# Spreads of attention weights as pairs of 32 x 64 matmuls, with a second copy of the values whose images are swapped

## The chip, the cores and the metric

The kernel runs on one core of one Trainium2 chip. The metric is the time of an execution on the device in microseconds (us); what is quoted is the median of several runs.

## The reference, cut to what matters

Two layers on x of 4 images, 64 channels, 32 x 32 pixels. The first is a deformable attention with 8 heads and 4 points:

```
v = (q @ W_value + b_value).reshape(B, Nq, HEADS, d)
off = (q @ W_off + b_off).reshape(B, Nq, HEADS, LEVELS, POINTS, 2)
attn = softmax(q @ W_attn + b_attn) over the 4 points
loc = ref + off / norm;  ix = loc_x * W - 0.5;  iy = loc_y * H - 0.5
sampled = bilinear samples of v at (ix, iy), zero outside
out = (sampled * attn).sum over points
out = out @ W_out + b_out + q
```

The second is a 3 x 3 convolution of the signs of its result with the signs of the weights (times their mean size), a batch normalization over all pixels, a residual and a PReLU. The signs need the whole attention, and the normalization needs the whole convolution.

## The kernel before, in words

Two images share the 128 partitions (PAIR = 2, 64 channels each), so there are G = 2 groups; `yh` is the upper or lower half of the pixels, 512 each. Offsets are small, so each pixel samples among 4 x 4 neighbours. A **tap** is one neighbour of one half: t from 0 to 31, in rows of four (row n = t // 4, the neighbour's line; column t % 4). For each tap:

- `attend` (VectorE, once a row) multiplies the turned probabilities by the vertical hat: `ps_ay`, in PSUM. ScalarE's `copy_ay` brings it to SBUF as `ays`.
- `weight` multiplies `ays` by the horizontal hat: the tap's weight, 128 rows (group, image, head, point) by 512 pixels. GpSimd makes 30 of the 32 (line 754, tile `ap`, four buffers), VectorE the first two (tile `a`).
- `spread` (TensorE, line 431) sums the points and copies each head's weight to its 8 channels, by four matmuls with 0/1 matrices, one per group and image. Each reads 64 rows, of which 32 are of its image. It writes `ps_w`, two buffers of two banks. For group 1 the images come out crossed, and `vpad` holds the values crossed too.
- `product` (VectorE, line 850) multiplies by the shifted window of the padded values `vpad`: `prod`, 8 buffers.
- a **unit** of `project` (TensorE, line 451) applies W_out and adds into `ps_out`: the unit of a tap, or ("sum", n), the sum of two products of a row that GpSimd's `pair_sum` makes with an adding DMA (line 760).

Every engine runs its own list in the order of the program; semaphores join them. TensorE's list has spread t, then what `UNITS_AFTER[t]` names, then spread t + 1. `carry_x` (line 444) starts an accumulation with x itself, once a half, and `turn` (line 419) transposes the probabilities. After the last unit ScalarE makes the signs of the lower half (line 680), TensorE convolves (line 483), VectorE takes statistics, and ScalarE, VectorE and GpSimd make the result. A flag (line 544) tells whether an offset was too large for 16 taps; it isn't here.

Of the kernel before, what the change touches and what calls it, by code (L numbers as in the profile page):

```python
# [20 lines left out]
PAIR = 2  # L21
G = B // PAIR
P = PAIR * C
YH = 2
# [12 lines left out]
SUMMED = range(ROWS - 1)  # L37
# [65 lines left out]
def deformable_attention_then_binary_conv(nc, x, const, w_in, w_out, params, w_conv, w_abs, out):  # L103
    ctx = ExitStack()
    with ctx:
# [35 lines left out]
        PR = 8  # L141
# [4 lines left out]
        flag = sb("flag", [1, 2])  # L146
# [30 lines left out]
        ps_flag = bank[6]  # L177
# [16 lines left out]
        s_vlow = sem("lower_values_stored")  # L194
        s_pos = sem("position_parts_ready")
# [9 lines left out]
        s_att = sem("probs_turned")  # L205
        s_ay = sem("ay_ready")
        s_a = sem("tap_weights_ready")
        s_ayc = sem("ay_copied")
# [72 lines left out]
        def v_window(g, yh, ky, kx):  # L281
# [44 lines left out]
        def units_of(n):  # L326

            first = TAPS * n
            if n == ROWS - 1:
                return [("tap", t) for t in range(first, first + TAPS)]  # L330
            return [("tap", first + 2), ("tap", first + 3), ("sum", n)]

        UNITS_AFTER = {6: [("tap", 2), ("tap", 3)], 7: [("sum", 0)], 17: [("tap", 15), ("sum", 3)], 18: [], 20: [],
                       21: [("tap", 18), ("tap", 19)], 31: [("tap", 28), ("tap", 29)]}
        for n in range(2, ROWS):
            for column in range(3):
                UNITS_AFTER.setdefault(TAPS * n + column, units_of(n - 1)[column:column + 1])
        UNITS = [unit for n in range(ROWS) for unit in units_of(n)]
        UPPER_UNITS = sum(len(units_of(n)) for n in range(TAPS))
# [11 lines left out]
        def quadrant(i, g):  # L351

            return slice(i * C, (i + 1) * C), slice((i ^ g) * C, (i ^ g) * C + C)
# [28 lines left out]
        def _(pe):  # L382
# [32 lines left out]
            def turn(yh):  # L415

                pe.wait_ge(s_prob, yh + 1)
                for n in range(NCH):
                    mm = pe.transpose(ps_att[:, n * P:(n + 1) * P], prob[:, yh, n * P:(n + 1) * P], cst[:, c_eye:c_eye + P])  # L419
# [103 lines left out]
            for t in range(NT * YH):  # L523
# [10 lines left out]
                if t == NT + 4:  # L534
                    carry_x(1)
# [510 lines left out]
```

## Time and profile before

| | us |
|---|---|
| median of 3 runs | 95.57 (95.44 to 96.04) |
| profiled execution | 95.7 |
| its span in the trace | 93.9 |
| TensorE busy | 76.6 |
| VectorE busy | 65.0 |
| GpSimd busy | 51.0 |
| ScalarE busy | 47.9 |

The span is what the trace covers; the profiled execution's time is 1.8 us more. PE is TensorE (PEld its weight loads), DVE VectorE, ACT ScalarE, POOL GpSimd, SP the sync engine, and a q behind a name its queue. In the trace each fp32 matmul shows as two records, so a spread's four matmuls are eight. A record of a matmul ends later than the next can begin (they are pipelined), so costs are taken from the distance between starts, or from the chain.

### The profile page before, as it was taken

To read this page: it belongs to the slowest core of one execution; us is meant where nothing else is said; L and a number is where in the kernel's file an instruction comes from. 1 tells how busy PE (TensorE), PEld (TensorE's weight loads), DVE (VectorE), ACT (ScalarE), POOL (GpSimd) and SP (SyncE) were. 2 spreads that over 40 slices of the span, in tenths; PEclk is the share of its full clock that TensorE was granted. 3 is DMA by queue.
4 is the path that set the end of the run, shared out by engine and by line. 5 is a ranking of instruction groups with operands and counts; after the bars stand their busy time and mean duration, and the time that the engine had idled before them with its cause. 6 is when DMAs were issued, how large, how long until landed. Compare 5 with 4: busy or idle time off the path is not lost.

```text
span 93.9 us, 1689 instructions
## 1 busy us (share of the span) xinstructions
PE 76.6 (82%) x648; PEld 33.0 (35%) x648; DVE 65.0 (69%) x81; ACT 47.9 (51%) x76; POOL 51.0 (54%) x47
## 2 busy tenths in 40 slices
PE   5999799879999999999997799999999999220000
PEld 4547074112246544333331355333333345010000
DVE  2624695995999664987973954997776408659930
ACT  2200899988689990399708950220000039419900
POOL 7920000059999999999998568899800000005000
PEclk9999999999999999999999999999999999996555
DMA  1998000000083083470924700910910000000095
GB/s 27 249 358 327 6 0 0 0 0 7 0 168 56 0 168 63 82 141 0 178 49 84 143 7 3 194 30 0 195 35 0 0 7 0 0 0 0 14 257 180
DMA packets 3209, 7.10 MB, mean 76 GB/s; under 512 B 512, under 2 KB 1024, under 8 KB 3200
## 3 DMA queue, kind: packets, MB, share of 16 engines
q0 software_dynamic: 1008, 3.67, 20.6%
q1 hardware_dynamic: 1904, 2.89, 9.8%
q10 hardware_dynamic: 288, 0.43, 1.5%
q8 instruction: 5, 0.08, 0.4%
q14 instruction: 4, 0.03, 0.1%
HBM read 2.27 MB, written 1.05 MB: 35 GB/s over the span
## 4 chain that ended last, share of the span: by engine, by line
PE 67%; ACT 15%; DVE 7%; issue 4%; POOL 3%; ACTq 1%; DVEq 0%; POOLq 0%
PE banks L431 27%; PE banks L451 23%; PE banks L444 4%; ACT tab L609 3%; ACT hat L614 3%; PE banks L483 3%; PE banks L501 3%; POOL ap L754 2%; ACT prod L734 2%; PE banks L404 2%; PE banks L396 2%; ACT prod L736 2%; DVE bns L957 1%; ACT sg L680 1%; ACT u L602 1%
## 5 line engine op out<-in xcount | busy, mean ns | idle before, releaser
L754 POOL TENSOR_TENSOR ap<-ays,hat 128x512 f32<-128x512 f32 x30 | 40.4, 1564 | 17.4 <-ACT ays L623 15.7
L850 DVE TENSOR_TENSOR prod<-banks,vpad 128x1024 f32<-128x1024 f32 (+1 forms) x33 | 38.6, 1187 | 11.7 <-PE banks L431 11.7
L431 PE MATMUL banks<-ap,cst 64*64 64x512 f32 x240 | 33.9, 596 | 1.3 <-DVE prod L850 1.1
L451 PE MATMUL banks<-prod,wo 64*64 64x512 f32 x200 | 27.8, 590 | 0.0
L431 PEld LDWEIGHTS banks<-ap,cst 64*64 64x64 f32 x240 | 10.1, 132 | 17.2 <-issue 9.4
L451 PEld LDWEIGHTS banks<-prod,wo 64*64 64x64 f32 x200 | 9.9, 133 | 11.5 <-issue 9.6
L779 POOL TENSOR_SCALAR prod<-prod,prm,st 128x512 f32<-128x512 f32 x2 | 1.5, 768 | 17.7 <-ACT st L728 17.7
L623 ACT ACTIVATE ays<-banks 128x512 f32<-128x512 f32 x8 | 4.7, 588 | 9.9 <-DVE banks L822 9.9
L609 ACT ACTIVATE tab<-u,cst 128x1024 f32<-128x1024 f32 x8 | 8.9, 1141 | 0.2
L680 ACT ACTIVATE sg<-banks,st 128x512 bf16<-128x512 f32 x2 | 1.3, 687 | 14.9 <-PE banks L451 14.9
L614 ACT ACTIVATE hat<-tab 128x1024 f32<-128x1024 f32 x8 | 8.3, 1050 | 0.1
L760 POOL DMA_DIRECT2D prod<-prod x7 | 7.5, 1077 | 0.4 <-issue 0.4
L822 DVE TENSOR_TENSOR banks<-banks,hat 128x512 f32<-128x512 f32 x8 | 5.5, 691 | 0.9 <-PE banks L419 0.9
L483 PE MATMUL banks<-sg,wcb 64*64 64x512 bf16 (+2 forms) x84 | 4.6, 350 | 0.2 <-ACT sg L680 0.2
L404 PEld LDWEIGHTS banks<-win,xs 128*128 128x128 f32 x32 | 3.9, 196 | 1.1 <-issue 1.1
L635 ACT ACTIVATE ex<-lsub 128x512 f32<-128x512 f32 x1 | 0.6, 631 | 6.9 <-DVE lsub L791 6.9
L390 PE MATMUL banks<-xs,win 128*64 128x512 f32 x16 | 4.1, 611 | 0.0
L404 PE MATMUL banks<-win,xs 128*128 128x64 f32 x32 | 4.0, 277 | 0.0
L444 PE MATMUL banks<-xs,cst 64*64 64x512 f32 x16 | 3.8, 590 | 0.0
L501 PE MATMUL banks<-ones 128*128 128x256 f32 x6 | 2.9, 661 | 1.0 <-POOL ones L742 1.0
L396 PE MATMUL banks<-prm,top_ones 128*128 128x512 f32 x4 | 3.0, 846 | 0.7 <-ACT u L602 0.7
L787 DVE TENSOR_REDUCE lmax<-banks 128x128 f32<-128x512 f32 x2 | 1.4, 686 | 3.1 <-PE banks L404 3.1
(81 smaller groups left out, 74.0 us busy)
## 6 DMA issues: line engine op xcount, KB each, us to landing
prod<-prod POOLq DMA_DIRECT2D x7, 512.0 KB, 4.8
xs<-x_dram SPq DMA_DIRECT2D x3, 256.0 KB, 4.9
out_dram<-prod SPq DMA_DIRECT2D x4, 128.0 KB, 2.6
out_dram<-prod SPq DMA_DIRECT2D x2, 256.0 KB, 2.6
wcf<-w_conv_dram SPq DMA_DIRECT2D x1, 288.0 KB, 5.2
wab<-w_abs_dram SPq DMA_DIRECT2D x1, 288.0 KB, 5.2
xs<-x_dram ACTq DMA_DIRECT2D x1, 256.0 KB, 4.1
cst<-const_dram SPq DMA_DIRECT2D x1, 227.0 KB, 5.0
```

What stands on the lines that cost most here:

```text
L404: mm = pe.matmul(ps_log[yh][:, at:at + C], xs[:, g, q:q + P], wp[:, 2, :], start=False, stop=(n == NCH - 1 and g == G - 1), skip_group_che ...
L431: mm = pe.matmul(ps_w[t % 2][rows_out, g, :], sel_of(g)[rows_in, rows_out], weights_at(t)[rows_in], start=True, stop=True)
L444: mm = pe.matmul(ps_out[g][rows_of_i], cst[rows_of_i, c_eye + i * C:c_eye + (i + 1) * C], chunk(xs, g, yh)[rows_of_i], start=True, stop=Fa ...
L451: mm = pe.matmul(ps_out[g][rows_out], wo[rows_in, rows_in], source[rows_in, g, :], start=False, stop=last, skip_group_check=True)
L483: mm = pe.matmul(ps_y[yh][g][rows_out, first_row * W:last_row * W], wcb[rows_in, ky * K + kx, :], sg[rows_in, g, y0:y0 + last_row - first_ ...
L501: pe.matmul(bank[6][:, 0:2 * P], ones[:], ones[:].unsqueeze(1).to_broadcast([P, 2, P]), start=True, stop=True)
L609: nc.scalar.activation(tab[:, n % 2], u[:, :, yh, :], ACT.Abs, bias=cst[:, c_tap + k:c_tap + k + 1]).then_inc(s_abs, 1)
L614: nc.scalar.activation(hat[:, yh, :, k, :], tab[:, n % 2], ACT.Relu, bias=1.0, scale=-1.0).then_inc(s_hat, 1)
L754: pool.tensor_tensor(ap[:, j % RAP, :], ays[:, t // TAPS % RY, :], hat[:, yh, 0, kx, :], ALU.mult).then_inc(s_ap, 1)
L760: pool.dma_start(prod[:, t % PR], prod[:, (t + 1) % PR], accum_op=ALU.add).then_inc(s_s2[n % 2], 16)
L822: nc.vector.tensor_tensor(ps_ay[:], ps_att[:], hat[:, yh, 1, ORDER[row], :], ALU.mult).then_inc(s_ay, 1)
L850: nc.vector.tensor_tensor(by_half_row(prod[:, t % PR, g, :]), by_half_row(ps_w[t % 2][:, g, :]), v_window(g, yh, ky, kx), ALU.mult).then_i ...
```

## The change

- **Spreads**: each of the four matmuls of a tap reads only the 32 rows of its group and image, a 32 x 64 tile. Taps 2 to 29 go in pairs. The second tap of a pair is "swapped": its images come out in the other halves of the partitions, so that the eight matmuls of a pair have eight different tiles. Its product reads `vswap`, a copy of `vpad` with the halves exchanged, which SP's queue makes with four DMAs, and its unit projects by the other quadrants. Units of both kinds are told apart by `is_swapped`; where the kind changes TensorE waits for its last unit.
- `ps_w` has three buffers, `prod` twelve, `ays` three. Pair sums add columns 0 and 2 of rows 0 to 5. `UNITS_AFTER` is a new table, and `carry_x(1)` comes three taps later.
- **Row factors**: ScalarE copies the turned probabilities to SBUF (`att`) once per half; `attend` reads them there (but for row 0) and writes `ays` in SBUF; `copy_ay` is gone. `turn(1)` has a spread's PSUM buffer and goes in before spread 10, which waits for ScalarE's copy.
- The flag's sum is moved from VectorE at the end to ScalarE in the middle.

```diff
-SUMMED = range(ROWS - 1)
+SUMMED = range(ROWS - 2)
+SPREADS = [(0,), (1,)] + [(t, t + 1) for t in range(2, ROWS * TAPS - 2, 2)] + [(ROWS * TAPS - 2,), (ROWS * TAPS - 1,)]
+SWAPPED = [pair[1] for pair in SPREADS if len(pair) == 2]
+TURN_AFTER = 9
...
+        vswap = sb("vswap", [P, G, VP, 2, SEG])
...
-        RY = 2
+        RY = 3
         ays = sb("ays", [P, RY, HALF])
+        att = sb("att", [P, YH, HALF])
...
-        PR = 8
+        PR = 12
...
-        ps_w = [banks[0], banks[1]]
+        ps_w = [banks[0], banks[1], banks[3]]
+        NW = len(ps_w)
         ps_out = [bank[4], bank[5]]
-        ps_att = bank[6]
-        ps_ay = bank[7]
+        turn_slot = (TURN_AFTER + 1) % NW
+        ps_att = [bank[6], ps_w[turn_slot][:, 0, :]]
...
+            yh, ky, kx = tap_of(t)
             y0 = yh * RH + ky + yh
-            return vpad[:, g, y0:y0 + RH, :, kx:kx + HW].rearrange("p g y a x -> p g (y a) x")
+            return (vswap if t in SWAPPED else vpad)[:, g, y0:y0 + RH, :, kx:kx + HW].rearrange("p g y a x -> p g (y a) x")
...
+        UNITS_AFTER = {7: [("tap", 3)], 9: [("tap", 1), ("sum", 0)], 11: [("tap", 5), ("tap", 7)], 13: [("sum", 1)],
+                       15: [("tap", 9), ("tap", 11)], 17: [("sum", 2)], 19: [("tap", 13), ("tap", 15)], 21: [("sum", 3)],
+                       25: [("sum", 4)], 27: [("tap", 17), ("tap", 19), ("tap", 21)], 29: [("sum", 5), ("tap", 24)],
+                       30: [("tap", 23), ("tap", 25)], 31: [("tap", 27)]}
+        UNITS_AT_END = [("tap", 29), ("tap", 26), ("tap", 28), ("tap", 30), ("tap", 31)]
+        UNITS = [unit for t in sorted(UNITS_AFTER) for unit in UNITS_AFTER[t]] + UNITS_AT_END
+        UPPER_UNITS = UNITS.index(("sum", 3)) + 1
...
-        def quadrant(i, g):
-
-            return slice(i * C, (i + 1) * C), slice((i ^ g) * C, (i ^ g) * C + C)
+        def quadrant(i, g, swapped=False):
+
+            j = i ^ g ^ swapped
+            return slice(i * C, (i + 1) * C), slice(j * C, (j + 1) * C)
...
+            for yh in range(YH):
+                sp.wait_ge([s_vp, s_vlow][yh], 2)
+                at = slice(yh * VP // YH, (yh + 1) * VP // YH)
+                for i in range(PAIR):
+                    rows_in, rows_out = quadrant(i, 1)
+                    sp.dma_start(vswap[rows_out, :, at], vpad[rows_in, :, at]).then_inc(s_vswap[yh], 16)
...
+                if t == 2:
+                    pe.wait_ge(s_attc, 1)
+                if t == TURN_AFTER + 1:
+                    pe.wait_ge(s_attc, 2)
+                if t >= NW:
+                    pe.wait_ge(s_p, products_done(t - NW, G - 1))
                 for g in range(G):
-                    rows_in = slice(g * C, (g + 1) * C)
                     for i in range(PAIR):
-                        rows_out = slice(i * C, (i + 1) * C)
-                        mm = pe.matmul(ps_w[t % 2][rows_out, g, :], sel_of(g)[rows_in, rows_out], weights_at(t)[rows_in],
+                        rows_in = slice(g * C + i * HP, g * C + (i + 1) * HP)
+                        lhs = cst[rows_in, c_sel + g * P + (i ^ g) * C:c_sel + g * P + (i ^ g) * C + C]
+                        mm = pe.matmul(ps_w[t % NW][quadrant(i, g, t in SWAPPED)[1], g, :], lhs, weights_at(t)[rows_in],
...
+                    pe.wait_ge(s_ov, 4)
+                    pe.matmul(ps_flag[0:1, 0:4], ones[:, 0:1], over_sum[:], start=True, stop=True).then_inc(s_fps, 1)
...
+                swapped = is_swapped(unit)
+                at = UNITS.index(unit)
+                if at and is_swapped(UNITS[at - 1]) != swapped:
+                    pe.wait_ge(s_acc, at)
+                mm = project_image(source, swapped, 0, last)
...
-            for t in range(NT * YH):
-                spread(t)
+            for taps in SPREADS:
+                for t in taps:
+                    spread(t)
...
-                if t == NT + 4:
+                if t == TURN_AFTER:
+                    pe.wait_ge(s_p, products_done(t + 1 - NW, G - 1))
+                    turn(1)
+                if t == NT + 7:
...
-                if t == 2 * TAPS + 1:
-                    pe.wait_ge(s_ay, TAPS)
-                    turn(1)
-                if t == 28:
-                    pe.wait_ge(s_ov, 4)
-                    pe.wait_ge(s_ay, ROWS)
-                    pe.matmul(ps_flag[0:1, 0:4], ones[:, 0:1], over_sum[:], start=True, stop=True).then_inc(s_fps, 1)
...
-            def copy_ay(n):
-
-                act.wait_ge(s_ay, n + 1)
-                if n == 0:
-                    act.wait_ge(s_a, DVE_COLUMNS[0])
-                if n >= RY:
-                    act.wait_ge(s_ap, sum(TAPS - c for c in DVE_COLUMNS[:n - RY + 1]))
-                nc.scalar.activation(ays[:, n % RY, :], ps_ay[:], ACT.Identity).then_inc(s_ayc, 1)
+            def copy_turned(yh):
+
+                act.wait_ge(s_att, yh + 1)
+                if yh == 0:
+                    act.wait_ge(s_ay, 1)
+                nc.scalar.activation(att[:, yh, :], ps_att[yh][:], ACT.Identity).then_inc(s_attc, 1)
...
+            act.wait_ge(s_fps, 1)
+            nc.scalar.activation(flag[:, 4:8], ps_flag[0:1, 0:4], ACT.Identity, accum_out=flag[:, 0:1]).then_inc(s_f1, 1)
...
-                pool.wait_ge(s_ayc, t // TAPS + 1)
+                pool.wait_ge(s_ay, t // TAPS + 1)
...
-                pool.wait_ge(s_p, products_done(t + 1, G - 1))
-                pool.dma_start(prod[:, t % PR], prod[:, (t + 1) % PR], accum_op=ALU.add).then_inc(s_s2[n % 2], 16)
+                pool.wait_ge(s_p, products_done(t + 2, G - 1))
+                pool.dma_start(prod[:, t % PR], prod[:, (t + 2) % PR], accum_op=ALU.add).then_inc(s_s2[n % 2], 16)
...
-                dve.wait_ge(s_att, yh + 1)
                 if n:
-                    dve.wait_ge(s_ayc, n)
+                    dve.wait_ge(s_attc, yh + 1)
+                    source = att[:, yh, :]
+                else:
+                    dve.wait_ge(s_att, 1)
+                    source = ps_att[0][:]
+                if n >= RY:
+                    dve.wait_ge(s_ap, sum(TAPS - c for c in DVE_COLUMNS[:n - RY + 1]))
                 wait_for_hat(dve, yh, ORDER[row])
-                nc.vector.tensor_tensor(ps_ay[:], ps_att[:], hat[:, yh, 1, ORDER[row], :], ALU.mult).then_inc(s_ay, 1)
+                nc.vector.tensor_tensor(ays[:, n % RY, :], source, hat[:, yh, 1, ORDER[row], :], ALU.mult).then_inc(s_ay, 1)
...
+                if t in SWAPPED:
+                    dve.wait_ge(s_vswap[0], 16 * PAIR)
+                    if yh or ky == TAPS - 1:
+                        dve.wait_ge(s_vswap[1], 16 * PAIR)
...
-                    nc.vector.tensor_tensor(by_half_row(prod[:, t % PR, g, :]), by_half_row(ps_w[t % 2][:, g, :]),
-                                            v_window(g, yh, ky, kx), ALU.mult).then_inc(s_p, 1)
+                    nc.vector.tensor_tensor(by_half_row(prod[:, t % PR, g, :]), by_half_row(ps_w[t % NW][:, g, :]),
+                                            v_window(t, g), ALU.mult).then_inc(s_p, 1)
```

TensorE's list around the last spreads, before (MATMUL x4 is one tap's spread at L431 or one unit at L451):

```order
L451 MATMUL banks<-prod,wo 64x512 x4
L431 MATMUL banks<-ap,cst 64x512 x4
L451 MATMUL banks<-prod,wo 64x512 x4
L431 MATMUL banks<-ap,cst 64x512 x4
L451 MATMUL banks<-prod,wo 64x512 x12
L483 MATMUL banks<-sg,wcb 64x512 x12
L451 MATMUL banks<-prod,wo 64x512 x4
```

The same place in the changed kernel, from the pair (26,27) on (spreads at L453, units at L477, the convolution at L513):

```order
L453 MATMUL banks<-ap,cst 64x512 x8
L477 MATMUL banks<-prod,wo 64x512 x12
L453 MATMUL banks<-ap,cst 64x512 x8
L477 MATMUL banks<-prod,wo 64x512 x8
L453 MATMUL banks<-ap,cst 64x512 x4
L477 MATMUL banks<-prod,wo 64x512 x8
L453 MATMUL banks<-ap,cst 64x512 x4
L477 MATMUL banks<-prod,wo 64x512 x20
L513 MATMUL banks<-sg,wcb 64x512 x12
L477 MATMUL banks<-prod,wo 64x512 x4
```

Between the last spread and the convolution stand three units before, five now, and two units stand ahead of that spread where there was one.

VectorE's list in rows 1 and 2, before (products at L850, `attend` at L822):

```order
L850 TENSOR_TENSOR prod<-banks,vpad 128x1024
L822 TENSOR_TENSOR banks<-banks,hat 128x512
L850 TENSOR_TENSOR prod<-banks,vpad 128x1024 x2
L796 TENSOR_REDUCE lsum<-ex 128x128
L822 TENSOR_TENSOR banks<-banks,hat 128x512
```

And in the changed kernel (products at L878, `attend` at L849), with what each waits for:

```order
L878 TENSOR_TENSOR prod<-banks,vpad 128x1024 [waits spread_ready]
L849 TENSOR_TENSOR ays<-att,hat 128x512 [waits hats_ready,turned_probs_copied]
L878 TENSOR_TENSOR prod<-banks,vpad 128x1024 [waits spread_ready]
L878 TENSOR_TENSOR prod<-banks,vswap 128x1024 [waits spread_ready,swapped_upper_values_in]
L818 TENSOR_REDUCE lsum<-ex 128x128 [waits exp_ready]
L849 TENSOR_TENSOR ays<-att,hat 128x512 [waits hats_ready,turned_probs_copied]
```

The places of `attend` stay; its operands move from PSUM to SBUF, and every second product reads `vswap`.

## Rows read from the trace of the kernel before

**Rows 1.** The page: busy time and share per engine, chain that ended last by engine and line.
```profile
PE 76.6 (82%) x648; PEld 33.0 (35%) x648; DVE 65.0 (69%) x81; ACT 47.9 (51%) x76; POOL 51.0 (54%) x47
...
PE 67%; ACT 15%; DVE 7%; issue 4%; POOL 3%; ACTq 1%; DVEq 0%; POOLq 0%
PE banks L431 27%; PE banks L451 23%; PE banks L444 4%; ACT tab L609 3%; ACT hat L614 3%; PE banks L483 3%; PE banks L501 3%; POOL ap L754 2%; ACT prod L734 2%; PE banks L404 2%; PE banks L396 2%; ACT prod L736 2%; DVE bns L957 1%; ACT sg L680 1%; ACT u L602 1%
```

**Rows 2.** Waits: engine and line, released by, us in total, times, longest.
```profile
DVE prod L850 <- PE banks L431: 11.7, 17, 1.9
...
PEld banks L431 <- POOL ap L754: 7.5, 11, 1.9
```

**Rows 3.** The chain in time: start us, us, what; fp32 spreads and units are x8.
```profile
22.44 1.09 PE banks L431 x8
...
26.10 1.72 PE banks L444 x8
...
34.69 0.86 PE banks L451 x8
35.55 0.59 PE banks L419 x4
36.14 1.02 PE banks L431 x8
...
75.04 0.66 PE banks L483 x12
75.70 0.93 PE banks L451 x8
...
76.65 0.58 ACT sg L680
```

**Rows 4.** GpSimd's timeline: start us, us, instruction; in brackets idle time before it.
```profile
19.87 5.00 POOL L754 TENSOR_TENSOR ap<-ays,hat 128x512 f32<-128x512 f32 x4 [14.64 <-ACT ays L623]
24.81 1.00 POOL L760 DMA_DIRECT2D prod<-prod  x1
...
28.08 1.33 POOL L771 TENSOR_TENSOR prob<-ex,lrec 128x512 f32<-128x512 f32 x1
29.14 2.74 POOL L754 TENSOR_TENSOR ap<-ays,hat 128x512 f32<-128x512 f32 x2
...
37.15 1.41 POOL L760 DMA_DIRECT2D prod<-prod  x1
37.76 5.80 POOL L754 TENSOR_TENSOR ap<-ays,hat 128x512 f32<-128x512 f32 x4
...
50.48 2.50 POOL L754 TENSOR_TENSOR ap<-ays,hat 128x512 f32<-128x512 f32 x2 [0.26 <-PE banks L431]
```

**Rows 5.** VectorE's timeline, the same columns.
```profile
12.20 0.69 DVE L805 TENSOR_TENSOR prob<-ex,lrec 128x512 f32<-128x512 f32 x1
...
22.36 2.46 DVE L850 TENSOR_TENSOR prod<-banks,vpad 128x1024 f32<-128x1024 f32 x2 [0.96 <-PE banks L431]
...
27.06 0.94 DVE L800 RECIPROCAL lrec<-lsum 128x128 f32<-128x128 f32 x1
...
37.29 1.23 DVE L850 TENSOR_TENSOR prod<-banks,vpad 128x1024 f32<-128x1024 f32 x1 [1.23 <-PE banks L431]
38.44 0.69 DVE L822 TENSOR_TENSOR banks<-banks,hat 128x512 f32<-128x512 f32 x1
39.03 2.35 DVE L850 TENSOR_TENSOR prod<-banks,vpad 128x1024 f32<-128x1024 f32 x2
```

**Rows 6.** Timeline of all engines, 2.8 to 5.6 us: VectorE's cast beside GpSimd's memset.
```profile
3.19 2.07 DVE L862 CAST pos_b<-prm 128x32 bf16<-128x32 f32 x1 [1.80 <-DMA prm<-params_dram]
3.20 2.02 POOL L744 MEMSET sg<- 128x2312 bf16 x1
```

**Rows 7.** The page: DMA issues, KB each, us to landing.
```profile
xs<-x_dram SPq DMA_DIRECT2D x3, 256.0 KB, 4.9
```

**Rows 8.** Window: us, busy time (instructions) of PE, PEld, DVE, ACT, POOL, granted clock, DMA.
```profile
50.30:67.80 17.50, 16.43 (x144) 6.64 (x136) 13.36 (x13) 6.21 (x15) 14.41 (x12) 1.00 0.45 86
```

More of the change, by code:

```diff
@@ L145, in deformable_attention_then_binary_conv @@
         overs = sb("overs", [P, 2, HALF])
-        flag = sb("flag", [1, 2])
+        flag = sb("flag", [1, 8])
         flagi = sb("flagi", [1, 1], I32)
@@ L176, in deformable_attention_then_binary_conv @@
         ps_log = [bank[7], bank[4]]
-        ps_flag = bank[6]
+        ps_flag = bank[4]
         ps_pair = bank[4]
@@ L324, in products_done, with is_swapped, last_read @@
             return t + 1 + (g if t == NT * YH - 1 else 0)
[L326 to L339, printed above, removed]
+        def is_swapped(unit):
+            return unit[0] == "tap" and unit[1] in SWAPPED
+        def last_read(t):
+            row, column = divmod(t, TAPS)
+            if row in SUMMED and column == 0:
+                return ("sum", row)
+            return ("tap", t)
+        UNITS_AFTER = {7: [("tap", 3)], 9: [("tap", 1), ("sum", 0)], 11: [("tap", 5), ("tap", 7)], 13: [("sum", 1)],
[5 more added lines that the diff above has]
+        UPPER_UNITS = UNITS.index(("sum", 3)) + 1
         def units_done(unit, g=G - 1):
@@ L440, in carry_x @@
                     pe.wait_ge(s_x1, 2)
-                for g in range(G):
+                    pe.wait_ge(s_ov, 4)
+                    pe.matmul(ps_flag[0:1, 0:4], ones[:, 0:1], over_sum[:], start=True, stop=True).then_inc(s_fps, 1)
+                for g in reversed(range(G)):
+                    if yh and g == 0:
+                        pe.wait_ge(s_f1, 1)
                     for i in range(PAIR):
@@ L446, in carry_x, with project_image @@
                 mm.then_inc(s_carry, 1)
-            def project_image(source, g, last):
+            def project_image(source, swapped, g, last):
                 for i in range(PAIR):
-                    rows_in, rows_out = quadrant(i, g)
+                    rows_in, rows_out = quadrant(i, g, swapped)
                     mm = pe.matmul(ps_out[g][rows_out], wo[rows_in, rows_in], source[rows_in, g, :], start=False, stop=last,
@@ L473, in project @@
                     pe.wait_ge(s_p, products_done(n, 1))
-                project_image(source, 1, last).then_inc(s_acc, 1)
+                project_image(source, swapped, 1, last).then_inc(s_acc, 1)
             def convolve_row(yh, ky, first_row, last_row):
@@ L537, in _ @@
                     project(unit)
-                if t == 2 * TAPS + 1:
-                    pe.wait_ge(s_ay, TAPS)
-                    turn(1)
-                if t == 28:
-                    pe.wait_ge(s_ov, 4)
-                    pe.wait_ge(s_ay, ROWS)
-                    pe.matmul(ps_flag[0:1, 0:4], ones[:, 0:1], over_sum[:], start=True, stop=True).then_inc(s_fps, 1)
-            project(UNITS[-2])
-            pe.wait_ge(s_f1, 1)
+            for unit in UNITS_AT_END[:-1]:
+                project(unit)
+            pe.wait_ge(s_p, products_done(NT * YH - 3, G - 1))
             pe.wait_ge(s_wc, 1)
@@ L766, in _ @@
                     weight(TAPS * (n + 1) + column)
-                    if column == 1:
+                    if column == 2 and n in SUMMED:
                         pair_sum(n)
@@ L830, in weight @@
                     dve.wait_ge(s_w, taps_of(False)[i - RA] + 1)
-                nc.vector.tensor_tensor(a[:, i % RA, :], ps_ay[:], hat[:, yh, 0, kx, :], ALU.mult).then_inc(s_a, 1)
+                nc.vector.tensor_tensor(a[:, i % RA, :], ays[:, t // TAPS % RY, :], hat[:, yh, 0, kx, :], ALU.mult).then_inc(s_a, 1)
             def product(t):
@@ L836, in product @@
                     dve.wait_ge(s_vlow, 2)
+                if t in SWAPPED:
+                    dve.wait_ge(s_vswap[0], 16 * PAIR)
+                    if yh or ky == TAPS - 1:
+                        dve.wait_ge(s_vswap[1], 16 * PAIR)
                 if t >= PR:
                     old = t - PR
[L839 to L844 removed]
+                    row, column = divmod(old, TAPS)
+                    if row in SUMMED and column == 2:
+                        dve.wait_ge(s_s2[row % 2], 16 * (row // 2 + 1))
                     else:
[L846 removed]
+                        dve.wait_ge(s_acc, units_done(last_read(old)))
                 dve.wait_ge(s_w, t + 1)
```

30 lines of the change are left out of this document (6 added, 24 removed).

## The prediction

> **What bounds the kernel now.** I read the page first, for its busy shares and its chain [rows 1]: the tensor engine is busy for 82% of the span, carries 67% of the chain, and half of the chain is two lines, the spreads (L431) and the projections of `project` (L451). Then the waits, for who feeds whom [rows 2]: VectorE waits 11.7 us for spreads, TensorE's weight loads wait 7.5 us for GpSimd's `ap`. Then the chain in time [rows 3]. One spread of a tap is 8 records in 0.86 us, one projected unit is 8 records in 0.86 us, and `carry_x` is 1.72 us, since its two images use the same two quadrants. From 22.44 to 76.65 us (the first `sign` of the lower half) the chain is almost only these. After that comes a tail of 95.7 − 76.65 = 19.05 us that the change leaves alone; the profiled execution took 95.7 us, 0.13 over the median of the runs, and my sum is made against it.
>
> Two other engines are close behind. GpSimd's stretch [rows 4]: four tap weights from 19.87 to the DMA issue at 24.81, 1.235 us each; the issue of a pair sum costs it 0.61 (37.15 to 37.76); `prob` of the lower half costs 1.06 (28.08 to 29.14). It runs without a gap until some 50 us, then the row at 50.48 shows that it waits for TensorE. VectorE [rows 5]: a product costs 1.15 (its step 37.29 to 38.44), `attend` 0.60 (38.44 to 39.03), the reciprocal at most 0.94. A row of four taps thus asks 6.9 us of TensorE, 4 x 1.235 + 0.61 = 5.55 of GpSimd and 5.2 of VectorE. Taking TensorE away buys at most the distance to GpSimd.
>
> **The change, part by part.**
>
> *Spreads in pairs.* 32 spreads become 14 pairs and 4 single ones. Each of the eight matmuls of a pair has a tile of 32 rows by 64 columns of its own. Nothing in the trace is 32 rows high. The nearest rows: with 64 x 64 tiles the four matmuls of a spread, and the four of a unit, fit in 0.86 us [rows 3], while `carry_x`, which has two tiles for four matmuls, takes 1.72. So time goes with matmuls per tile, and rows that share row groups but not columns do run together. Bounds for a pair: 0.86 and 1.72. I take 0.86, by the nearest rows. Instructions are no limit: the convolution's 12 matmuls take 0.66 us (0.055 each, with as many weight loads), and a pair has 16 in 0.86.
> Here the Trainium skill speaks against the change. TensorEngine Tiling (Array Packing), Restrictions and Gotchas, says that different row tiles cannot access the same PSUM bank simultaneously; a pair has two row tiles per bank, in different halves of the partitions. This case's rows differ from it: a unit does just that with row tiles 0 and 64 and still takes 0.86. By the page the pairs gain nothing (that time is a rival, below).
>
> *Changes of tile size.* Units stay at 64 x 64, so each block of spreads now has a change of mode before and after it. Nearest rows: the spread after the transposes takes 1.02 instead of 0.86 [rows 3]. Bounds per change: 0 and 0.16; I take 0.10.
>
> *Units.* One more, 26 for 25 (six pair sums, not seven), and they are moved. The order after pair (28,29) decides: the order of the program shows sum 5, tap 24, spread 30, taps 23 and 25, spread 31, taps 27, 29, 26, 28, 30, a quarter of the convolution, tap 31. That is 12 blocks of 0.86 (the pair, spreads 30 and 31, nine units) = 10.32, + 0.66 + 0.93 (the convolution's row and the last unit, [rows 3]) + 5 changes x 0.10 = 12.4 us from the start of that pair to `sign`. Until then TensorE has slack: from 22.44 on, 13 pairs 11.2, values 0.86, two carries 3.44, transposes 0.59, 16 units 13.8 and some 27 changes 2.7 are 32.6 us, which would reach pair (28,29) at 55.0. So its start is set by another engine. Where projection flips between straight and swapped units it waits for its own last unit; all but one flip have a spread or the transposes between them, and that one costs a matmul's latency, which I leave in the range.
>
> *GpSimd's path to weight 29.* From 19.87: 28 weights x 1.235 = 34.6, `prob` 1.06, six issues x 0.61 = 3.66: 59.2 us. The start stays: the hat and the copy that delay it now [rows 4] give way to the same hat behind a copy of the turned probabilities.
>
> *`attend` through SBUF.* The eight products `ays` = probabilities x hat read PSUM and write PSUM today, and ScalarE copies each (an engine that is busy for half of the span, [rows 1]). Seven of them will now read two SBUF tensors while GpSimd works. On VectorE alone this costs nothing: `prob`, with both inputs in SBUF, takes 0.69 like them [rows 5]. But a cast of 128 x 32 elements, with input and output in SBUF, took 2.07 us, from 3.19 to the end of GpSimd's memset (3.20 to 5.22) [rows 6]: the two engines can lock each other out of SBUF for a whole instruction. The trace has no VectorE instruction with two SBUF inputs beside GpSimd's weights. Bounds: 0, or 0.60 of GpSimd's time per `attend` and up to one weight's 1.235 of VectorE's. I take the lock, with 7 x 0.60 = 4.2 us on GpSimd: weight 29 is then done at 63.4.
> The Trainium skill's page SBUF — State Buffer, Who interferes with whom, says that a VectorE instruction with two SBUF inputs contends with a GpSimd instruction that reads SBUF, as an exclusive lock; the cast agrees with the lock, but was an instruction of another kind.
>
> *VectorE's path.* From product 2 at 22.36: 25 products to product 26 28.8, six attends 3.6, sum (as an attend) and reciprocal 1.5: 56.3; waits of half a weight at each attend, 3.7, make 60.0. There is one stall: spread 10 now waits for `turn(1)`, its copy, and two units: 0.14 + 0.59 + 1.72 + 0.2 + 0.86 + 0.14 = 3.65 us after product 7, with products 8 and 9 (2.3) to cover it, so 1.4 open. That gives 61.4, under GpSimd's 63.4, so it is covered there; if not, it is 1.4 more.
>
> *Costing nothing.* `vswap` is filled by SP's queue, four DMAs of 64 partitions: the upper half may start some 2 us behind `prob` (12.20, [rows 5]) and a DMA of 256 KB lands in 4.9 [rows 7], so before product 3, at 23.5 now; if it took twice as long, VectorE would wait about 1. The lower half is wanted only ten products later. The flag moves off VectorE to ScalarE and TensorE in the middle, where both have time. The third PSUM buffer and the twelve `prod` buffers only loosen waits. The clock was granted in full from 50.3 to 67.8 [rows 8], with TensorE busy for 94% (16.43 of 17.50 us); I expect it to stay, with idle gaps of about 1 us.
>
> **Sum.** 63.4 + 0.05 + 12.4 = 75.9 us for `sign`, against 76.65: 0.8 earlier, **94.9 us**. Its own range: 92.8, if half of the lock's 4.2 falls into waits that GpSimd has anyway, to 96.6 (stall uncovered, changes at 0.16).
>
> **Rivals.**
> No lock (0.30): GpSimd reaches 59.2, the stall stays open since its four buffers are then full: 59.2 + 1.4 + 0.05 + 12.4 = 73.0, 3.6 earlier, 92.1. For it: the cast is no evidence for this form. Against: GpSimd reads SBUF all the time.
> `attend` starved (0.15): GpSimd's weights follow one another without a gap, and if the next one takes the port each time, an attend waits a weight and a half, 1.85 us. Then VectorE is the bound: 22.4 + 28.8 + 6 x (0.60 + 1.85) + 1.5 + 1.4 = 68.8, + 12.45 = 81.25, 100.3 us, slower. It decides from a wait of 1.0 us per attend on. Against it: GpSimd must stop by itself when its buffers are full.
> No sharing in pairs (0.07), which is also the case that the change does not do what it says, and what the page on tiling would give: TensorE stays the bound. From 22.44: 30 spreads 25.8, 26 units 22.4, values, carries and transposes 4.9, convolution and rest 0.7, 34 changes 3.4, and the 1.3 us of waits that the same sum leaves over in the profile shown (52.9 against 54.2): 80.9, or 100.0 us.
> 0.02 is for what I have not seen.
>
> **From cases to numbers.** A change of 1% (94.6 to 96.5) is about what can be told. Faster: all of no lock and a third of the forecast, 0.46. Same: six tenths of the forecast, 0.28. Slower: the two rivals, some of the forecast and the rest, 0.26. For 8 in 10 the range reaches down past no lock, 91.6, and up into the first third of the slow rivals, 98.5.
>
> **What would show it.** Right: a pair is 16 records in about 0.86 us; the spread line's 27% of the chain falls by a half and more; VectorE's `attend` records have a mean over 0.9 us, or GpSimd's weights beside them are longer than 1.24; the last weight ends near 66; from pair (28,29) to `sign` 12.4 us of nearly gapless TensorE. Wrong: `attend` at 0.69 and undisturbed weights (no lock); waits of 1.5 us at `attend` and GpSimd idle behind them (starved); a pair of 1.7 us (no sharing); VectorE idle before product 3 (the swap lands late).

## The result, and the profile after

Slower: a median of 101.89 us (100.29 to 102.49, 4 runs) against 95.50 (95.36 to 96.04) for the kernel before on the same chip. The ratio is 1.054, with a 95% interval of 1.049 to 1.058. The forecast was 94.9 us, in a range to 98.5. Medians here are over all executions and ratios leave out those that some disturbance made longer, often at a lower granted clock (for the changed kernel two of the four are left, 100.29 and 101.32 us, with spans of 98.5); the profiled execution, at 102.46 us, is not one of these and has a span of 99.6, so what follows rests on its order of events and not on its last microsecond.

First the page, its busy time per engine, to be held against [rows 1]:

```profile
PE 77.6 (78%) x656; PEld 26.2 (26%) x656; DVE 71.2 (71%) x80; ACT 45.0 (45%) x72; POOL 51.0 (51%) x46
...
PE 47%; ACT 14%; DVE 13%; issue 11%; POOL 9%; ACTq 1%; DVEq 0%; POOLq 0%
```

TensorE's share of the chain fell from 67% to 47%, and that of the spread line from 27% to 15%, less than the half that was forecast; VectorE's rose from 7% to 13%, and `issue` from 4% to 11%. VectorE is busy for 6.2 us more, though it does no more work. The costliest groups on the page say where (line, engine, operation, shapes, count, busy us, mean ns):

```profile
L453 PE MATMUL banks<-ap,cst 32*64 32x512 f32 x240 | 24.8, 640 | 5.8 <-DVE prod L878 4.0
...
L849 DVE TENSOR_TENSOR ays<-att,hat 128x512 f32<-128x512 f32 x7 | 11.8, 1693 | 0.0
```

Spreads are 9 us of busy time cheaper (24.8 for 33.9). The seven `attend` of two SBUF inputs have a mean of 1.69 us, where 0.69 is their own length. The mean hides two kinds. VectorE's timeline of the changed kernel (start us, us, instruction; idle time before it in brackets):

```profile
38.92 3.90 DVE L849 TENSOR_TENSOR ays<-att,hat 128x512 f32<-128x512 f32 x1
...
47.26 0.67 DVE L849 TENSOR_TENSOR ays<-att,hat 128x512 f32<-128x512 f32 x1
```

Five of seven take 0.67 to 1.22 us; two take 3.90 and 3.45 (below). The instructions of both engines around a quick one at 53.92, taken one by one:

```profile
53.05 1.27 POOL L776 TENSOR_TENSOR ap<-ays,hat 128x512 f32<-128x512 f32 x1
53.92 0.95 DVE L849 TENSOR_TENSOR ays<-att,hat 128x512 f32<-128x512 f32 x1
54.30 0.88 POOL L782 DMA_DIRECT2D prod<-prod  x1
```

and around the slow one at 59.42:

```profile
58.62 1.55 POOL L776 TENSOR_TENSOR ap<-ays,hat 128x512 f32<-128x512 f32 x1
59.42 3.45 DVE L849 TENSOR_TENSOR ays<-att,hat 128x512 f32<-128x512 f32 x1
59.84 1.16 POOL L782 DMA_DIRECT2D prod<-prod  x1
60.45 1.86 POOL L776 TENSOR_TENSOR ap<-ays,hat 128x512 f32<-128x512 f32 x1
...
62.95 1.27 POOL L776 TENSOR_TENSOR ap<-ays,hat 128x512 f32<-128x512 f32 x1 [0.64 <-DVE ays L849]
```

The quick one ends 0.55 us after GpSimd's weight does (54.32): it gets the port at the end of the instruction that held it. The slow one sits through the rest of a weight, a DMA issue and another weight, and ends at 62.87, 0.56 us after GpSimd has stopped at 62.31 because it wants the very factor that this `attend` makes. The two differ in GpSimd's records before them: 1.27 us, the next one starting 0.02 before the end, or 1.55 us, the next one starting 0.33 before the end. The one of 3.90 is of the slow kind too: GpSimd's records ahead of it overlap by 0.31, and it ends at 42.81, 0.56 after GpSimd has stopped (42.26).

The end of the chain of the changed kernel, from its last full pair to the signs of the lower half (start us, us, what), answers to [rows 3]:

```profile
64.15 1.09 PE banks L453 x8
...
65.28 1.09 PE banks L453 x8
66.37 2.74 PE banks L477 x24
69.10 1.04 PE banks L453 x16
70.14 1.88 PE banks L477 x16
72.02 1.02 PE banks L453 x8
73.04 1.88 PE banks L477 x16
74.92 1.02 PE banks L453 x8
75.94 1.92 PE banks L477 x16
77.86 0.14 issue
77.99 2.81 PE banks L477 x24
80.80 0.66 PE banks L513 x12
81.46 0.92 PE banks L477 x8
...
82.40 0.58 ACT sg L704
```

A pair is 16 records in 1.04 us. The signs come at 82.40 instead of 76.65, 5.75 us later, and that is the loss; some 1 us of it belongs to a fall of TensorE's clock in this execution (see the clock, below). The pair (26,27) at 64.15 is not one: spread 27 starts 1.13 after spread 26, when product 24 has freed its buffer. This is VectorE's backlog behind the `attend` of 3.45 us.

### The profile page after: what moved, and what is told of

Read it like the earlier page. It is cut to its first block, busy times and chain, and to the rows that moved or that the text cites. A ratio compares the mean times of both kernels' runs of the same rounds, so it can differ in the third digit from the quotient of the medians.

```text
span 99.6 us, 1718 instructions
## 1 busy us (share of the span) xinstructions
PE 77.6 (78%) x656; PEld 26.2 (26%) x656; DVE 71.2 (71%) x80; ACT 45.0 (45%) x72; POOL 51.0 (51%) x46
## 3 DMA queue, kind: packets, MB, share of 16 engines
HBM read 2.27 MB, written 1.05 MB: 33 GB/s over the span
## 4 chain that ended last, share of the span: by engine, by line
PE 47%; ACT 14%; DVE 13%; issue 11%; POOL 9%; ACTq 1%; DVEq 0%; POOLq 0%
PE banks L477 17%; PE banks L453 15%; POOL ap L776 9%; DVE ays L849 4%; DVE prod L878 4%; ACT tab L637 3%; ACT hat L642 3%; PE banks L513 3%; PE banks L531 3%; ACT prod L756 2%; PE banks L422 2%; PE banks L470 2%; PE banks L414 2%; ACT prod L758 1%; DVE bns L982 1%
## 5 line engine op out<-in xcount | busy, mean ns | idle before, releaser
L453 PE MATMUL banks<-ap,cst 32*64 32x512 f32 x240 | 24.8, 640 | 5.8 <-DVE prod L878 4.0
L878 DVE TENSOR_TENSOR prod<-banks,vpad 128x1024 f32<-128x1024 f32 (+1 forms) x19 | 21.9, 1159 | 8.3 <-PE banks L453 8.3
L477 PE MATMUL banks<-prod,wo 64*64 64x512 f32 x208 | 26.0, 608 | 0.2 <-PE banks L477 0.2
L878 DVE TENSOR_TENSOR prod<-banks,vswap 128x1024 f32<-128x1024 f32 x14 | 16.9, 1208 | 0.7 <-PE banks L453 0.5
L849 DVE TENSOR_TENSOR ays<-att,hat 128x512 f32<-128x512 f32 x7 | 11.8, 1693 | 0.0
L477 PEld LDWEIGHTS banks<-prod,wo 64*64 64x64 f32 x208 | 6.9, 135 | 18.0 <-issue 12.5
L453 PEld LDWEIGHTS banks<-ap,cst 32*64 32x64 f32 x240 | 5.4, 132 | 23.6 <-issue 12.7
L782 POOL DMA_DIRECT2D prod<-prod x6 | 5.9, 989 | 0.3 <-DVE prod L878 0.3
L916 DVE TENSOR_SCALAR x<-banks,prm 128x512 f32<-128x512 f32 x1 | 0.8, 750 | 5.7 <-ACT sg L704 5.7
L513 PE MATMUL banks<-sg,wcb 64*64 64x512 bf16 (+2 forms) x84 | 4.6, 350 | 0.2 <-ACT sg L704 0.2
L649 ACT ACTIVATE att<-banks 128x512 f32<-128x512 f32 x2 | 1.2, 586 | 6.3 <-PE banks L437 6.3
```

Of the source, the lines that this page charges most:

```text
L453: mm = pe.matmul(ps_w[t % NW][quadrant(i, g, t in SWAPPED)[1], g, :], lhs, weights_at(t)[rows_in], start=True, stop=True)
L477: mm = pe.matmul(ps_out[g][rows_out], wo[rows_in, rows_in], source[rows_in, g, :], start=False, stop=last, skip_group_check=True)
L513: mm = pe.matmul(ps_y[yh][g][rows_out, first_row * W:last_row * W], wcb[rows_in, ky * K + kx, :], sg[rows_in, g, y0:y0 + last_row - first_ ...
L782: pool.dma_start(prod[:, t % PR], prod[:, (t + 2) % PR], accum_op=ALU.add).then_inc(s_s2[n % 2], 16)
L849: nc.vector.tensor_tensor(ays[:, n % RY, :], source, hat[:, yh, 1, ORDER[row], :], ALU.mult).then_inc(s_ay, 1)
L878: nc.vector.tensor_tensor(by_half_row(prod[:, t % PR, g, :]), by_half_row(ps_w[t % NW][:, g, :]), v_window(t, g), ALU.mult).then_inc(s_p, 1)
```

## The experiments

Theory A: the second SBUF input makes `attend` wait for the port that GpSimd's weights hold, and it can starve. Theory B: TensorE's new costs (changes of tile size, pairs that don't overlap, more units after the last spread) make the loss. Ratios are to the kernel before on the same chip, with a 95% interval; where two runs are compared, the difference of their ratios is given, in percent of the time of the kernel before.

**One SBUF input.** `attend` at the same place, of the same length and with the same waits, but without the vertical hat, so with one input in SBUF:

```diff
-                nc.vector.tensor_tensor(ays[:, n % RY, :], source, hat[:, yh, 1, ORDER[row], :], ALU.mult).then_inc(s_ay, 1)
+                if n:
+                    nc.vector.tensor_reduce(ays[:, n % RY, :], source.unsqueeze(2), AX.X, ALU.add).then_inc(s_ay, 1)
```

> The changed kernel, but attend(1) to attend(7) are a sum over an axis of length 1 of the turned probabilities: one SBUF input instead of two, the same size, place and waits. The vertical hat is left out of the rows' factors 1 to 7. Starved attends (VectorE waits for the SBUF port that GpSimd holds): all attends at 0.69 us, the two of 3.90 and 3.45 us gone, the signs some 5 us earlier, 95 to 96 us. TensorE bounds it (tile changes, pairs that start one after the other, six units after the last spread): attends shorter, but the time stays above 99.

Measured: 95.05 us, ratio 0.986 (0.982 to 0.991), all seven at 0.67 or 0.68 us, the signs at 75.51. Theory A stands: the form of seven instructions is worth 6.7% (1.054 to 0.986 before rounding), more than the whole loss. From pair (28,29) to the signs it still takes 13.3 us (62.21 to 75.51), so B's costs are real but are no loss against before.

**No adding DMAs.**

```diff
-                pool.dma_start(prod[:, t % PR], prod[:, (t + 2) % PR], accum_op=ALU.add).then_inc(s_s2[n % 2], 16)
+                pool.sem_inc(s_s2[n % 2], 16)
```

> The changed kernel without the six adding DMAs: GpSimd only counts the semaphore up, so the product of column 2 of rows 0 to 5 is left out of the sum. If an attend is passed over until GpSimd stops by itself, the two long attends stay at 3 us and more. If it is passed over only where a DMA issue follows a weight at once, none is above 1.9 (one weight and itself), and the time falls to about 96 to 97.

Measured: 95.23 us, ratio 0.996 (0.992 to 1.000). No `attend` is above 1.22 us, though GpSimd's weights follow one another from 30 to 57 us with no gap above 0.06. (The time says less than the attends do, since the run also spares GpSimd six issues of 0.61 us.) Instructions of both engines around one of them:

```profile
48.72 1.28 POOL L776 TENSOR_TENSOR ap<-ays,hat 128x512 f32<-128x512 f32 x1
49.60 0.96 DVE L849 TENSOR_TENSOR ays<-att,hat 128x512 f32<-128x512 f32 x1
49.95 1.73 POOL L776 TENSOR_TENSOR ap<-ays,hat 128x512 f32<-128x512 f32 x1
```

So a VectorE instruction does get in at the end of a weight that runs in step with its neighbours, as they all do without DMA issues: it ends at 50.56, 0.56 after the weight, and GpSimd's next weight, which is then kept waiting, takes 1.73 instead of 1.28. This is the fair exchange that the prediction assumed everywhere.

**GpSimd yields before it issues a sum.**

```diff
+                if n:
+                    pool.wait_ge(s_ay, n + 3)
```

> The changed kernel, but from the second pair sum on GpSimd waits, before it issues the sum, until the attend behind the same product is done. Starved attends: none above 1.9 us, the two long ones lose 2 us and 1.6 us, the time falls by about 3 us to 97 to 98. If TensorE bounds it, or if the pause costs GpSimd as much as VectorE gains: no change, 100 to 101.

Measured: 100.98 us, ratio 1.055 (1.050 to 1.060): nothing gained. My expectation missed: the four attends that GpSimd paused for took 1.77, 2.52, 2.50 and 2.50, three of them above 1.9. Around one:

```profile
44.68 1.56 POOL L776 TENSOR_TENSOR ap<-ays,hat 128x512 f32<-128x512 f32 x1
45.51 2.52 DVE L851 TENSOR_TENSOR ays<-att,hat 128x512 f32<-128x512 f32 x1
45.91 1.55 POOL L776 TENSOR_TENSOR ap<-ays,hat 128x512 f32<-128x512 f32 x1
...
48.57 0.87 POOL L784 DMA_DIRECT2D prod<-prod  x1 [1.11 <-DVE ays L851]
```

Here no DMA issue lies between the two weights, and yet `attend` is passed over at their border (45.91) and gets in only when GpSimd pauses (47.46; it ends 0.57 later). So an issue right behind a weight is not what passes `attend` over. Compared with the run before, what differs is the overlap: records of 1.55 that start 0.33 before the one ahead has ended. That gave the next experiment.

**Weights brought back into step.** Once a row, behind a DMA issue, a weight waits for the completion of the weight before it:

```diff
+                if t >= TAPS and t % TAPS == 0:
+                    pool.wait_ge(s_ap, j)
```

> The changed kernel, but from row 1 on the weight of column 0, the second behind each DMA issue, waits until the weight before it is complete. Theory: behind a DMA issue GpSimd's weights overlap one another by 0.3 us (records of 1.55 instead of 1.27) until it idles once, and while they overlap it never lets the SBUF port go. Then here the records are 1.27 again after that wait, every attend gets in at the next weight's end (under 1.9 us, none above 3), and the time falls by 3 to 4 us, to 97 to 98, with some 0.4 us lost per row on GpSimd. Rival: an attend just loses to whatever GpSimd has queued; then the two attends above 3 us stay, and the time too, 100 to 101.

Measured: 99.38 us, ratio 1.038 (1.032 to 1.044). The attends take 0.84, 1.39, 0.82, 0.71, 0.68, 0.84 and 0.81 us: none starves. Around the one that took 3.90 before:

```profile
34.99 1.56 POOL L778 TENSOR_TENSOR ap<-ays,hat 128x512 f32<-128x512 f32 x1
36.68 1.28 POOL L778 TENSOR_TENSOR ap<-ays,hat 128x512 f32<-128x512 f32 x1
...
37.91 1.28 POOL L778 TENSOR_TENSOR ap<-ays,hat 128x512 f32<-128x512 f32 x1
39.03 0.71 DVE L851 TENSOR_TENSOR ays<-att,hat 128x512 f32<-128x512 f32 x1
39.15 1.74 POOL L778 TENSOR_TENSOR ap<-ays,hat 128x512 f32<-128x512 f32 x1
```

One wait turns 1.56 into 1.28, and the port is let go. The time falls by 1.6% only, not by the 3 to 4 us expected, since GpSimd is now the bound: from 30.26 to 67.45 it stands still only for the pauses that were put in. Its timeline of the same run:

```profile
40.84 0.86 POOL L784 DMA_DIRECT2D prod<-prod  x1
41.44 5.93 POOL L778 TENSOR_TENSOR ap<-ays,hat 128x512 f32<-128x512 f32 x4
47.33 0.85 POOL L784 DMA_DIRECT2D prod<-prod  x1
```

A row takes it 6.49 us (40.84 to 47.33), where it can do 5.55: 0.46 for the `attend` that it lets in (1.74 for 1.28), 0.45 for the pause (36.68 − 34.99 = 1.69 instead of 1.24).

**One part alone, in the kernel before.** Row factors through SBUF as in the change, nothing else of it:

```diff
+                nc.scalar.activation(att[:, yh, :], ps_att[:], ACT.Identity).then_inc(s_ayc, 1)
...
-                nc.vector.tensor_tensor(ps_ay[:], ps_att[:], hat[:, yh, 1, ORDER[row], :], ALU.mult).then_inc(s_ay, 1)
+                nc.vector.tensor_tensor(ays[:, n % RY, :], source, hat[:, yh, 1, ORDER[row], :], ALU.mult).then_inc(s_ay, 1)
```

> The kernel before with one part of the change alone: ScalarE copies the turned probabilities once per half, attend reads them in SBUF and writes the factor in SBUF. Starved attends: some attends of 2 us and more here too; since TensorE is the bound and has a backlog, part of it is covered: 1 to 3 us slower than before. If the form costs nothing beside GpSimd: within 0.5 of before, attends at 0.69.

Measured: 103.77 us (102.13 to 103.85) against 95.79, 6 to 8 us slower: more than I expected, and more than the whole change loses. Its attends take 3.58 and 3.72 us where those of the change took 1.22 and 3.90, and I expected TensorE's backlog to cover part of it. It covers next to nothing: over the 0.69 of each, the seven attends wait 7.2 us, and the signs come at 84.62, 7.97 us later than before. Part of that is the clock: behind the second long `attend` it was granted at 0.50 from 46.68 to 50.09, and a spread and a unit took 1.99 and 1.66 us instead of 1.09 and 0.86.

**The same, but read from PSUM.** `source` is the turned probabilities in PSUM, and ScalarE copies nothing:

```diff
-                if n:
-                    dve.wait_ge(s_ayc, yh + 1)
-                    source = att[:, yh, :]
-                else:
-                    dve.wait_ge(s_att, 1)
-                    source = ps_att[:]
+                dve.wait_ge(s_att, yh + 1)
+                source = ps_att[:]
```

> The kernel before with factors written to SBUF by attend as in the run with SBUF factors only, but read from the probabilities in PSUM, so with one SBUF input; no copies by ScalarE at all. If the second SBUF input made that run 8 us slower: attends at 0.69 and the time of before, 95 to 96, or up to 0.5 less since a factor reaches GpSimd 0.6 us earlier. If it was something else in the move (three buffers, waits): 98 and more.

Measured: 96.10 us, against 95.67, at a ratio of 0.995 (0.990 to 0.999). All attends from the second on take 0.68. From the run ahead it differs in the memory that one operand comes from, in ScalarE's two copies of 0.6 us, and in that `turn(1)` waits for the fourth `attend`, as before, and not for a copy. This is theory A in its plainest form.

**Spreads on 64 rows again**, once with the one-input attends, once as in the change:

```diff
-                        rows_in = slice(g * C + i * HP, g * C + (i + 1) * HP)
+                        rows_in = slice(g * C, (g + 1) * C)
```

> The run with one-input attends, but each spread matmul reads 64 rows again (64 x 64 tiles, the same order of work): no eight tiles at once, and no change of tile size between spreads and units. If pairs share the array as the prediction took it, a pair costs 1.72 instead of 1.04, 14 pairs cost 9.5 us more of TensorE, less 30 changes at 0.17 (5 us): 2 to 5 us slower than with 32 rows, 97 to 100. If pairs gain nothing (no sharing): some 3 to 5 us faster, 90 to 92. The vertical hat is left out as there.

> The changed kernel with the spreads on 64 x 64 tiles in the same order, attends as in the change. Gives the price of pairs while attends starve. If TensorE is not the bound there: within 1 us of the changed kernel (100 to 102). If it is: 103 and more.

Measured: 96.43 us, ratio 1.008 (1.005 to 1.011), against 0.986 with 32 rows: pairs of 32 x 64 tiles are worth 2.1%, some 2 us, the low end of the 2 to 5 us that I expected. With the attends of the change: 100.72 us, ratio 1.051 (1.042 to 1.059), the same as the change's 1.054 within the intervals; its attends starve like those of the change (4.05 and 3.48 us), and while they do, the tiles don't matter.

**All of the computation, factors from PSUM.** If the port alone is at fault, the change can be had without it. The factors of a half are made at once, while the probabilities still lie in PSUM:

```diff
-        RY = 3
+        RY = 8
...
+                dve.wait_ge(s_att, yh + 1)
+                source = ps_att[yh][:]
...
+                if t == 1:
+                    for n in range(1, TAPS):
+                        attend(n)
+                if t == TURN_AFTER - 1:
+                    for n in range(TAPS, ROWS):
+                        attend(n)
```

> The changed kernel with all of its computation, but the factors of a half are made at once, straight from the turned probabilities in PSUM: attends 1 to 3 behind product 1, attends 4 to 7 behind product 8, eight ays buffers, no att and no copies by ScalarE; spread 2 waits for attend 3 and spread 10 for attend 7. No VectorE instruction beside GpSimd's weights has two SBUF inputs. If the port alone made the change slower: attends at 0.69, the time of the run with one-input attends or a little less, ratio to before 0.97 to 0.99 (93 to 95). If what that run gained came from the hat that it left out, or if spread 10's wait for four attends (2.4 us) is not covered: 95.5 to 97.5.

Measured: 95.58 us, ratio 0.997 (0.994 to 1.000): 5.7% better than the change, but 1.1% short of the run with one-input attends, and so in the second of the two expected ranges. It is not the hat, since the attends take 0.68 or 0.69; it is that they come in batches. VectorE's timeline shows what the first batch costs:

```profile
20.65 1.88 DVE L833 TENSOR_TENSOR ays<-banks,hat 128x512 f32<-128x512 f32 x3
23.82 1.22 DVE L862 TENSOR_TENSOR prod<-banks,vpad 128x1024 f32<-128x1024 f32 x1 [1.29 <-PE banks L452]
```

Spread 2 waits for three attends, so product 2 starts at 23.82 instead of 22.36. Spread 10 waits for the second batch (its last `attend` ends at 36.66), and TensorE stands still from 36.02 to 36.76. What bounds it otherwise is TensorE's list: 13.3 us again from pair (28,29) to the signs (62.96 to 76.26).

**Taps 30 and 31 paired too**, with the last units in fewer blocks:

```diff
-                        25: [("sum", 4)], 27: [("tap", 17), ("tap", 19), ("tap", 21)], 29: [("sum", 5), ("tap", 24)],
-                        30: [("tap", 23), ("tap", 25)], 31: [("tap", 27)]}
-        UNITS_AT_END = [("tap", 29), ("tap", 26), ("tap", 28), ("tap", 30), ("tap", 31)]
+                        25: [("sum", 4)], 27: [("tap", 17), ("tap", 19), ("tap", 21)], 29: [("sum", 5), ("tap", 24), ("tap", 26)],
+                        31: [("tap", 23), ("tap", 25), ("tap", 27), ("tap", 29)]}
+        UNITS_AT_END = [("tap", 28), ("tap", 30), ("tap", 31)]
```

> The run with all factors from PSUM, and taps 30 and 31 are a pair too (31 swapped), with the last units in fewer blocks. From pair (28,29) to the signs that run takes 13.3 us: three blocks of spreads at 1.02 to 1.04 and ten units in gaps. Here one block of spreads (1.04) and two changes of tile size (0.17 each) less: 12.0 us, so 1.2 us earlier, ratio to before 0.983 to 0.99. If TensorE were not the bound there (products set the end): less than 0.5 us earlier.

Measured: 94.58 us, ratio 0.990 (0.984 to 0.995): 1.0% under the kernel before and 6.4% under the changed one. Its chain to the signs:

```profile
63.01 1.04 PE banks L452 x16
64.05 2.74 PE banks L476 x24
66.78 1.04 PE banks L452 x16
67.83 3.64 PE banks L476 x32
...
71.60 1.95 PE banks L476 x16
...
75.18 0.58 ACT sg L694
```

12.2 us from the pair to the signs, 1.1 less, where 1.2 was worked out.

## Why the prediction was wrong

**The failed step is the sum's term for the lock at `attend`.** The prediction took "the lock, with 7 x 0.60 = 4.2 us on GpSimd", a wait of at most one weight's 1.235 us on VectorE, and GpSimd as the engine that sets pair (28,29) at 63.4. The lock is there, and its price on GpSimd was near where it is paid: 0.46 per attend in the run of weights brought into step. But the wait has no such bound. It ends at a weight's end only if GpSimd's instructions don't overlap, and behind each DMA issue they do, until GpSimd idles. Then the wait ends when GpSimd idles. All ten attends that met overlapping records show it (two in the change, four in the run where GpSimd yields, two with 64 rows, two in the kernel before with SBUF factors): each ends 0.55 or 0.56 us after the last record ahead of GpSimd's pause. Two of seven attends took 3.90 and 3.45 us, together 5.55 us more than twice the mean of the other five (0.90), so VectorE set the pace and the pair started at 69.1. In the terms of the sum, VectorE's path had 3.7 us for the waits at the six attends behind product 2; they were 6.9. The overlap stood in the rows that I had: two weights cover 2.74 us from 29.14, behind a DMA issue, and 2.50 from 50.48, behind a pause [rows 4]. The run with one SBUF input, which removes the lock and, beside it, only the hat, came out 6.7% lower.

**The rival "`attend` starved"** was that mechanism, with a chance of 0.15 and 100.3 us; two of the four executions took 100.3 and 101.3. Its sign came as well: GpSimd idle behind both long attends, 0.64 us each. Its price came out near by luck: it assumed 1.85 us at each of six attends, and the truth was two long waits and five short ones. The argument against it, that GpSimd stops by itself, is true and is the very way in which such a wait ends; I counted it as a protection when the stop comes only after GpSimd has run out of factors, that is, of VectorE's own work. The runs show a block of one instruction for weights in step (attends of 0.95 and 0.96 us, at the most 1.57) and of several for weights that overlap (3.90). The Trainium skill's page SBUF — State Buffer, SBUF: two separate sides, says that whichever engine starts first has the port for the whole instruction and that the other blocks; the trace agrees for the first kind, and for the second the block lasts longer than that.

**Pairs** were right in kind: a pair costs 1.04 us where two spreads cost 1.72, and the rival without sharing is out. The pairs, with two row tiles in each PSUM bank, ran together as the units did. By the Trainium skill's TensorEngine Tiling (Array Packing), Restrictions and Gotchas, different row tiles cannot access one PSUM bank simultaneously; the measurement decides. 1.04 is 0.18 over my 0.86; it holds a change of tile size.

**Changes of tile size** were taken at 0.10. A pair and two units take 1.04 + 1.88 = 2.92 against 3 x 0.86 = 2.58: 0.34 for two changes, 0.17 each, just over my upper bound of 0.16, if a pair itself costs 0.86. With 64 rows, where the size doesn't change, the two units take 1.72 and not 1.88. The flip of `is_swapped` within a block, left in the range, costs 0.14 of idle time and its drained pipe. In all 13.3 us from pair (28,29) to `sign` instead of 12.4.

**What I had not seen:** a pair is one block only if nothing holds up its second spread. Spread t + 1 waits for product t − 2, and behind the slow `attend` the pair (26,27) took 2.22 us (64.15 to 66.37). In the run with one SBUF input four pairs opened too, and there it was GpSimd's overlap: weight t + 1 is each time the first behind a DMA issue, and its record ends late. Its chain, and its weight 27 on GpSimd:

```profile
57.69 1.78 PE banks L453 x16
...
55.41 2.92 POOL L776 TENSOR_TENSOR ap<-ays,hat 128x512 f32<-128x512 f32 x1
```

The weight ends at 58.33 and spread 27 starts at 58.39; the other three took 1.77, 1.90 and 1.89. From pair (10,11) to pair (28,29) this run has six pairs at 1.04 and these four, 13.6 us, where with 64 rows the same ten take 17.2. Of the 3.6 us saved 2.1 are given back, by count at the 14 other changes of tile size (an estimate: 0.15 each), and the signs come 1.5 us earlier (75.51 for 77.01). That is why pairs are worth 2 us and not the 9 that 14 x 0.68 would give.

**The clock** was expected to stay. In the profiled execution it didn't. Windows of the changed kernel, in the columns of [rows 8]:

```profile
41.68:44.09 2.41, 0.00 (x0) 0.03 (x1) 2.41 (x3) 2.35 (x5) 1.77 (x2) 1.00 1.00 192
44.35:47.76 3.41, 3.41 (x20) 0.64 (x16) 3.41 (x4) 3.21 (x9) 2.45 (x3) 0.50 0.00 0
```

TensorE stood idle for 2.41 us, waiting for product 11 behind the `attend` of 3.90; then it was granted half of its clock (1.2 of 2.4 GHz) for 3.41 us. In the chain:

```profile
44.09 3.11 PE banks L453 x16
47.21 2.16 PE banks L477 x16
```

The two units take 1.88 at the full clock. VectorE then waited 1.45 us for spread 16. The change on 64 rows, whose attends starved for as long, kept the full clock there and had its signs at 81.35, 1.05 us earlier: an estimate of what the fall cost. The rest of the loss doesn't need it: the runs with 64 rows and with a GpSimd that yields lose 5% at the full clock.

**The stall at `turn(1)`** was worked out as 1.4 us; VectorE waited 2.19 us before product 10. The sum let `turn(1)` start 0.14 us after product 7. It started 1.07 after it, at 34.16, since spread 9, which lies ahead of it on TensorE, had waited for its weight until 33.08. The blocks behind it cost what the sum had within 0.1 us, and ScalarE's copy (34.85 to 35.45), which I had left out, was done before the two units were (36.62). Nothing was late in the copies of the values: product 3 started at 24.06, released by its spread, and the two DMAs that it needs had landed by 19.8 (the four took 3.8 to 7.3 us).

## What to carry to other kernels

When an operand of a VectorE instruction moves from PSUM to SBUF and GpSimd works from SBUF beside it, look first at whether the instruction now has two SBUF inputs; its own duration says nothing, and the wait need not end with the other engine's instruction. Look at GpSimd's records: where each starts well before the one ahead has ended (behind DMA issues of its own), such a wait lasts until GpSimd idles (3.90 and 3.45 us here, for an instruction of 0.69). And if GpSimd stops only for what VectorE makes, the two take turns at standing still.

## What the runs showed of the hardware

- GpSimd's overlap grows with each DMA issue and is lost when it idles: the weights' records are 1.27 or 1.28 us at a step of 1.24, then 1.55 behind one issue; in the run with one SBUF input, where GpSimd never idles, they reach 2.60 us behind five DMA issues, at the same step, and 2.67 to 2.92 behind the sixth. What waits for a weight waits for the end of its record. The row of the fifth:

```profile
53.59 2.60 POOL L776 TENSOR_TENSOR ap<-ays,hat 128x512 f32<-128x512 f32 x1
```

  The mean duration of such a group [rows 4] says nothing of GpSimd's pace. Why the overlap keeps the port is not shown; that ending it frees the port is.
- Eight matmuls on eight 32 x 64 tiles, two row tiles per PSUM bank in different halves of its partitions, run together: 1.04 us for a pair, where the same pair on 64 x 64 tiles takes 1.72. A change between 32 x 64 and 64 x 64 costs some 0.17 us (two units behind one take 1.88, and 1.72 without).
- TensorE's granted clock fell from 1.00 to 0.50 for 3.41 us after 2.41 us without a matmul (44.35 to 47.76), and in the kernel before with SBUF factors for as long (46.68 to 50.09), after 2.75 us without one. In the run with one SBUF input it stayed at 1.00 from 5.7 to 84.2 us.
- The part alone is dearer in the old kernel (103.77 us) than the whole change is in the new (101.89), though its attends wait as long (7.2 and 7.0 us over the 0.69 of each); its longest, 3.58 and 3.72 us, are also behind DMA issues. The signs are 8.0 us later than before in the one, and in the other 6.9 later than with one SBUF input, from where they stood 1.1 earlier than before. So half of the difference is what the rest of the change gains; the rest of it is not settled.
